# K's halves in DRAM: by feature with four heads side by side, loaded in two transfers instead of three

## The reference, cut to what matters

```python
def _heads(x):
    b, s, _ = x.shape
    return x.reshape(b, s, H, W).transpose(0, 2, 1, 3)
q = _heads(x_q @ Wq.T + bq)
k = _heads(x_k @ Wk.T + bk)
v = _heads(x_v @ Wv.T + bv)
scores = jnp.einsum('bhqw,bhkw->bhqk', q, k) / np.sqrt(W).astype(np.float32)
...
p = jax.nn.softmax(scores, axis=-1)
h = jnp.einsum('bhqk,bhkw->bhqw', p, v)
...
x = x + jnp.tanh(g_xattn[0]) * _L0_xattn_ref(_layernorm(x, axis=-1), ctx_1024, ctx_1024, mask_BxS2_ik0, ...)
x = x + jnp.tanh(g_ffn[0]) * _L0_ffn_ref(_layernorm(x, axis=-1), ...)
x = x + jnp.tanh(g_xattn[1]) * _L1_xattn_ref(_layernorm(x, axis=-1), ctx_1024, ctx_1024, ...)
x = x + jnp.tanh(g_ffn[1]) * _L1_ffn_ref(_layernorm(x, axis=-1), ...)
```

## Time and profile before

| | |
|---|---|
| median of 3 runs | 1571.54 us (1571.06 to 1573.1) |
| the profiled execution | 1573.01 us |
| its span, first to last instruction | 1570.1 us |
| granted TensorE clock, mean | 1.000 |
| DMA | 160,413 packets, 264.01 MB, mean 168 GB/s |
| KS<-kd (L762) | 192 transfers of 361.0 KB |
| kd<-ksh, kd<-ksl and first groups (L744) | 256 transfers of 192.0 or 169.0 KB |

### The profile page before, as it was taken

How to read it: one execution, slowest core, us unless ns; L and a number is a source line. 1 busy time by engine, 2 the same in 40 slices (tenths; PEclk the granted TensorE clock), 3 DMA queues, 4 the chain that set the end, 5 groups by cost and what they waited for, 6 DMA issues and landing times.

```text
span 1570.1 us, 25561 instructions
## 1 busy us (share of the span) xinstructions
PE 1556.6 (99%) x9226; PEld 1423.1 (91%) x9226; DVE 1024.0 (65%) x1814; ACT 963.7 (61%) x1994; POOL 426.9 (27%) x570
## 2 busy tenths in 40 slices
PE   9999999999999999999999999999999999999998
PEld 7999899999989999999999998889899989988755
DVE  6577887787786562223544335547777777778997
ACT  5676777777775455444544435447677767677665
POOL 4221222222235222222222223312211122122851
PEclk9999999999999999999999999999999999999999
DMA  7866767687583226554365652576676686668622
GB/s 244 193 171 165 201 181 195 163 204 184 137 219 100 95 81 202 177 186 161 104 228 194 210 176 83 181 182 182 165 199 169 163 195 173 164 159 215 213 52 59
DMA packets 160413, 264.01 MB, mean 168 GB/s; under 512 B 51549, under 2 KB 104413, under 8 KB 160148
## 3 DMA queue, kind: packets, MB, share of 16 engines
q1 hardware_dynamic: 159944, 261.97, 60.1%
q10 hardware_dynamic: 332, 0.23, 0.1%
HBM read 191.11 MB, written 58.57 MB: 159 GB/s over the span
## 4 chain that ended last, share of the span: by engine, by line
PE 93%; DVE 3%; ACT 2%; issue 1%; DMA 1%; POOL 0%; SPq 0%; DVEq 0%; ACTq 0%; POOLq 0%
PE ps L1249 33%; PE ps L881 16%; PE ps L885 14%; PE ps L981 8%; PE ps L959 8%; PE ps L1050 2%; PE ps L1186 2%; PE ps L901 2%; PE ps L943 2%; PE ps L948 2%; PE ps L1206 1%; PE ps L946 1%; PE ps L947 1%; ACT P L1967 1%; DVE nmax L1398 0%
## 5 line engine op out<-in xcount | busy, mean ns | idle before, releaser
L1249 PE MATMUL ps<-ah_f,wh_f 128*128 128x400 f32 x1288 | 442.0, 344 | 0.0
L1249 PE MATMUL ps<-al_f,wh_f 128*128 128x400 f32 x1288 | 441.3, 343 | 0.0
L2325 POOL TENSOR_TENSOR cxl<-raw,cxh 128x384 fp32r<-128x384 f32 (+1 forms) x112 | 105.6, 965 | 557.7 <-ACT cxh L1909 557.7
L1831 DVE TENSOR_TENSOR wl_f<-raw_f,wh_f 128x1024 fp32r<-128x1024 f32 x85 | 103.8, 1223 | 232.8 <-POOL wh_f L2315 232.8
L1398 DVE TENSOR_REDUCE nmax<-ps 100x1 f32<-100x722 f32 x256 | 220.9, 904 | 33.5 <-PE ps L947 30.0
L1249 PEld LDWEIGHTS ps<-al_f,wh_f 128*128 128x128 f32 x1288 | 242.2, 188 | 0.0
L1249 PEld LDWEIGHTS ps<-ah_f,wh_f 128*128 128x128 f32 x1288 | 241.9, 188 | 0.2
L1967 ACT ACTIVATE P<-ps,nmax 100x722 f32<-100x722 f32 x256 | 220.4, 864 | 28.1 <-DVE nmax L1398 27.9
L1979 ACT ACTIVATE PT<-ps 128x400 fp32r<-128x400 f32 x384 | 165.9, 505 | 70.5 <-PE ps L959 69.3
L2243 ACT ACTIVATE raw_f<-wl_f 128x1024 f32<-128x1024 f32 x88 | 93.5, 1062 | 174.1 <-DVE wl_f L1831 174.1
L1404 DVE TENSOR_TENSOR PT<-ps,PT 128x400 fp32r<-128x400 f32 x384 | 196.5, 568 | 3.2
(11 more groups left out here) (227 smaller groups left out, 2644.3 us busy)
## 6 DMA issues: line engine op xcount, KB each, us to landing
KS<-kd SPq DMA_DIRECT2D x192, 361.0 KB
raw_f<-in_h SPq DMA_DIRECT2D x64, 512.0 KB, 4.4
raw_f<-in_gud SPq DMA_DIRECT2D x48, 512.0 KB, 4.5
raw<-in_ctx SPq DMA_DIRECT2D x64, 192.0 KB, 3.6
raw_f<-in_w SPq DMA_DIRECT2D x24, 512.0 KB, 3.6
kd<-ksh SPq DMA_DIRECT2D x60, 192.0 KB, 2.1
kd<-ksl SPq DMA_DIRECT2D x60, 192.0 KB, 2.4
raw<-in_ctx SPq DMA_DIRECT2D x64, 169.0 KB, 4.2
```

What stands on the lines that cost most here:

```text
L1249: return e.matmul(o, p, q, start=start, stop=stop)
L1831: e.tensor_tensor(wl[:, z, :], raw[:, r, :], raw32(wh[:, z, :]), ALU.subtract).then_inc(v_ul, 1)
L2325: e.tensor_tensor(m.cx[1][:, k, off:off + n], m.raw[:, k, off:off + n], raw32(m.cx[0][:, k, off:off + n]), ALU.subtract).then_inc(g_cx, 1)
```

## The change

The DRAM tensor kd holds, for each of its four places, a part for the low half and one for the high half, and in each part the features of a head (32) come first, then the group's four heads, then the 722 columns. A store writes the 128 rows of ksh or ksl to four heads of 32 rows each; a row is 384 or 338 columns long, as before. The load to partitions 32 to 95 (low half, high half) is one transfer, the one to partitions 0 to 31 (high half) another; a partition's four heads follow each other in DRAM, 11,552 bytes. The count of a place's semaphore, `ks_done`, is lower by one transfer.

```diff
-        kd = nc.dram_tensor("kd", (4, 2, 128, T), F32, kind="Internal").ap()
+        kd = nc.dram_tensor("kd", (4, 2, W, 4, T), F32, kind="Internal").ap()
...
         def ks_done(L, m):
-            return 16 * ((4 if L == 0 else 3) * (m // 2 + 1) + (4 * 16 if L else 0))
+            return 16 * ((3 if L == 0 else 2) * (m // 2 + 1) + (3 * 16 if L else 0))
...
                 for c in range(2):
-                    e.dma_start(kd[n % 4, c][:, off:off + size],
+                    e.dma_start(kd[n % 4, 1 - c, :, :, off:off + size].rearrange("p j n -> j p n"),
                                 raw32(kst_of(m, b, g)[c][:, off:off + size])).then_inc(d_kd[half][n % 4], 16)
...
                 for half in range(2):
                     w.wait_ge(d_kd[half][n % 4], kd_done(L, n))
-                for r, c in enumerate((0, 1, 0)):
-                    e.dma_start(raw32(m.KS[32 * r:32 * r + 32, z, :, :]),
-                                kd[n % 4, c].rearrange("(j p) n -> p j n", j=4)).then_inc(d_ks[z], 16)
+                e.dma_start(raw32(m.KS[32:96, z, :, :]), kd[n % 4]).then_inc(d_ks[z], 16)
+                e.dma_start(raw32(m.KS[0:32, z, :, :]), kd[n % 4, 1]).then_inc(d_ks[z], 16)
```

## The result

The changed kernel takes 1808.23 us (median of 4 runs, 1804.69 to 1814.36) against 1571.54: ratio 1.151, 95% interval 1.1494 to 1.1526, 237 us slower. The forecast was 1670 us, with a range of 1600 to 1770: the direction was right, the size too small by 138 us. The profiled execution took 1809.53 us.

What follows compares the result with a forecast made beforehand. TensorE, busy 99%, bounds the kernel and would wait behind slow stores: 80 us in the batches plus 10 and 10 at the layers' starts make 100 us on a median of 1571.5, forecast 1670 us, range 1600 to 1770.

Steps and rivals of the forecast that it cites:

- What bounds the kernel: TensorE, busy for 99% of the span, bounds the kernel; its score matmuls never waited for a transfer into KS.
- four engines: K's stores (L744), to 4 heads of 32 rows, run on 4 of 16 engines: 8.2 us a group instead of 2.06.
- the dearer bound of 8.8: Store cost in us a group on four engines, by the rate of the 115-row store; 34 us on 1670.
- The load at 3.9 us: KS loads (L762) fall from 5.3 us an engine: two thirds at 361 GB/s (2.05), one third as before (1.77); gain hidden.
- The rival in which the load gains nothing: Stores on four engines, KS loads stay at 5.3 us instead of 3.9: 78 us more, 1750 us; chance 0.12.
- The starts: First scores of each layer come 10 us later, behind slow K stores; SyncE's mask wait in the first layer ends at 52.5.
- The places: ACT's overwrites of ksh and ksl wait for stores, 100 to 140 us in total; a first-layer batch takes 62 us.
- 2a, 3a and 3b: K jobs by group and column half (a 384, b 338); ACT's evictions there come 1.5, 2.7 and 5.8 us late.
- what "TensorE loses" a batch, 0.2 + 1.3 + 4.7 = 6.2 us: TensorE's loss at three late ACT evictions in a first-layer batch; 5.2 in the second layer; 80 us over seven batches each.
- the walk: One batch followed with the old kernel's issue times, transfers served in order on four engines; 6.2 us lost a batch.
- 3.8 us of cover: Lateness hidden before the next job on the eviction's PSUM bank: 1.3, 1.4 and 1.1 us at the three late evictions.
- The clock, priced at nothing: TensorE's granted clock was 1.00 in stretches read; no row showed what gaps near 5 us do; the upper end left room.

Runs made afterwards that it cites:

- two heads: Changed kernel with each store issued as two transfers of two heads (64 rows each, destination's outermost count 2): 2214.27 us, ratio 1.4088.
- rows in order: Changed kernel with K's weight columns and bias reordered ahead of the launch, so stores go 128 rows to 128 rows, same two loads: 1571.62 us, ratio 0.9999.
- The filled gaps: Changed kernel with unread TensorE matmuls of 112 columns where it idles, including 24 ahead of the scores that wait for KS: 1804.2 us, ratio 1.1482.
- made gaps: Kernel before the change, with TensorE made to wait once in each of 7 batches of either layer for small GpSimd writes: 1611.24 us, ratio 1.0252.
- stores by head: Changed kernel with each store of K's half issued as four transfers of one head (32 rows each), same two loads: 1704.42 us, ratio 1.0853.

## Why the prediction was right, and where it failed

- **What bounds the kernel, and four engines:** right. Stores alone show 0.27, and the runs with two heads and with rows in order bracket it. The price taken, 8.2 us a group, was a little low: by the first two windows (0.27 x 16 / 93 and / 86 GB/s, 46 to 50 engine-us a MB) it is 8.6 to 9.3, the dearer bound of 8.8, which the prediction priced at 34 us more.
- **The load at 3.9 us:** right (0.87 x 4.5), though its two terms, 2.05 and 1.77, add up to 3.8, and the agreement to the digit is luck. Right too that its gain is hidden: the run with rows in order gains nothing. The rival in which the load gains nothing gave 1750, nearer to the result, by a mechanism that the window refutes. The Trainium skill's advice (SBUF — State Buffer, "Summary: rules for kernel authors") to prefer 32 partitions over 64 does not hold for partitions 32 to 95: three loads of 32 took 5.0 us, and 24 us more in all.
- **The starts:** nearly right. SyncE's wait for the masks ended at 50.90 (forecast 52.5), the first scores came 13.9 us later in the first layer and, beyond the 131.2 us by which the feed-forward network between the layers had shifted, 9.1 later in the second (10 and 10).
- **The places:** right. ACT's L1919 is late at 2a, 3a and 3b, as walked (and by some 1 us on average at 1a); but it waits for 227 us in all, not 100 to 140, and a first-layer batch takes 72.3 us, not 62.
- **The failed step: what "TensorE loses" a batch, 0.2 + 1.3 + 4.7 = 6.2 us.** Measured are 16.2 in the first layer and, where 5.2 were forecast, 12.8 in the second. Three terms were off, here by the first layer's mean. First, the lateness at 2a, 3a and 3b: the walk had 10.0 us in all, the three steps grew by 3.6 + 2.4 + 8.1 = 14.1. The walk took the issue times from the kernel before; but an eviction that is late issues its own store late, and the next landing is later still. At 3b of the batch shown the pair needed 13 us from its issue (350.47) to the end of ACT's wait (363.52), not 9.3. SyncE in time and a window, kernel after:

```profile
345.39 0.57 SPq L761 DMA_DIRECT2D KS<-kd  x1
...
346.62 0.63 SPq L734 DMA_DIRECT2D traw<-in_ctxt  x1
347.30 0.53 SPq L695 DMA_DIRECT2D xs<-x  x1
350.47 0.57 SPq L744 DMA_DIRECT2D kd<-ksh  x1
...
351.00:357.50 6.50, 3.91 (x29) 3.56 (x27) 3.73 (x8) 2.98 (x7) 0.06 (x1) 1.00 0.51 122
```

Up to 357.50 the share of 0.51 is twice that of stores alone, so transfers issued ahead of the pair were still moving; only then does it stand at 0.25 (359.00, above). Which of them took the time was not tried. Second, the walk took off 3.8 us of cover, one share for each place, while the batch gave back 0.6 (3a to 2b). A likely reason, shown by no run, is that TensorE's slack is used up at the first stall and isn't there for the next. Third, the steps 0a to 1a and 3b to 0a, at which the walk had no loss, grew by 2.8; 1.1 of it came back when the gaps were filled and the clock stayed up.
- **The clock, priced at nothing:** no row showed it, and the upper end was to leave room. The profile after shows 78 us of longer TensorE time, and it is tempting to add them to 159 us of idle time and call 237 explained. The filled gaps say otherwise: with the clock at 0.980 instead of 0.952 the kernel is 4 us faster, 16 in the twelve batches and 11 lost outside them. That is net of what the added matmuls cost, so the clock's own share stays open; but the lost time mostly follows the stores, and the clock fell behind idle time that they had made. That TensorE's busy time and its idle time add up to the span is no more than arithmetic once another path sets the pace.
- **The range:** its top, 1770, was built from bounds of prices (load, store), and the measured prices lie at or near them. The error was in the model that used them, and nothing in the range stood for that.

## What to carry to other kernels

Before a layout in DRAM is changed, look at the outermost count of both sides of every transfer that touches it: 128 against 4 cut a store from 16 engines to 4 and cost 15%, and reordering the weights' columns ahead of the launch gave the same layout at no cost in device time. When a resource gets slow enough to be waited for, follow one whole period around (eviction, store, landing, next eviction), and let every lateness move the later issue times, instead of charging each stall once against the old times and taking its cover off. And test a suspected cause such as the clock by taking it away: here it looked like a third of the loss (78 of 237 us), and filling the gaps gave back 4 us, 16 in the batches where they were filled.

## What the runs showed of the hardware that was not expected

- A transfer to partitions 32 to 95 took 3.9 us an engine together with its neighbour of 32, against 5.0 for three of 32 with the same long rows.
- In the run with made gaps, all six of 2.28 to 3.89 us were followed by some 3 us at granted clock 0.50, and one of the two of 1.75 us; each fall cost TensorE 2.0 us. In the changed kernel a gap of 2.52 us left the clock at 1.00.
- An issue on SyncE took 0.45 us in the run with stores by head, so its transfers of 48 KB, issued one behind the other, can't pass some 109 GB/s (49,152 bytes in 0.45 us) on any number of engines; the window of stores alone had 102.
